# Graph attention on one core: where GpSimd issues late moves, adjacency loads and the accumulator base

## The reference

```python
h = relu(layernorm(x))
adj = maximum(adj, eye)
q, k, v = (einsum('nd,hdk->hnk', h, W) for W in (Wqs, Wks, Wvs))
scores = einsum('hqk,hmk->hqm', q, k) * 64 ** -0.5
scores = scores + 0.01 * eye - 1e16 * (1.0 - adj)
att = softmax(scores, axis=-1)
return x + einsum('hqm,hmk,hko->qo', att, v, Wo)
```

## Time and profile before

| | us |
|---|---|
| median of 3 runs | 2705.91 |
| lowest, highest | 2703.6, 2707.09 |
| the profiled execution's own time | 2709.6 |
| its span in the trace | 2708.1 |

### The profile page before, as it was taken

One profiled execution on the slowest core, in us unless ns is written; L12 is line 12 of the kernel. 1 busy time (PEld: TensorE's weight loads), 2 busy tenths in 40 slices (PEclk: granted clock), 3 DMA queues, 4 the chain that ended last, 5 costly groups with the idle time before them and its releaser, 6 DMA issues. The chain is left out here.

```text
span 2708.1 us, 58752 instructions
## 1 busy us (share of the span) xinstructions
PE 2630.7 (97%) x17344; PEld 1901.9 (70%) x17344; DVE 2253.6 (83%) x3833; ACT 1850.8 (68%) x3041; POOL 1280.6 (47%) x2418
## 2 busy tenths in 40 slices
PE   7899999999999999999998999999999999999997
PEld 5666777767777776766766777777777777777775
DVE  6788888888888888888847888888888888888885
ACT  3576777767767676776745777777777777777774
POOL 2356655566565556655512444444444444343433
PEclk9999999999999999999999999999999999999999
DMA  6367766677776677776652566656565656555654
GB/s 163 111 143 177 184 163 175 165 168 167 173 190 170 164 177 166 171 171 169 167 142 76 146 158 151 158 142 145 138 151 145 164 146 162 133 146 138 157 144 106
DMA packets 263358, 418.51 MB, mean 155 GB/s; under 512 B 98944, under 2 KB 119936, under 8 KB 259200
## 3 DMA queue, kind: packets, MB, share of 16 engines
q1 hardware_dynamic: 172032, 228.88, 33.0%
q0 software_dynamic: 89088, 184.69, 29.7%
q10 hardware_dynamic: 2176, 4.19, 0.4%
HBM read 136.31 MB, written 46.27 MB: 67 GB/s over the span
## 5 line engine op out<-in xcount | busy, mean ns | idle before, releaser
L307 POOL DMA_DIRECT2D S<-S x2048 | 1007.8, 500 | 1137.1 <-DVE S L723 1089.6
L702 DVE CUSTOM_DVE_ANT_0 S<-psS,B 128x1024 f32<-128x1024 f32 x1024 | 1228.4, 1218 | 268.3 <-PE psS L449 155.1
L589 ACT ACTIVATE S<-S,negm 128x1024 f32<-128x1024 f32 (+1 forms) x768 | 1095.8, 1428 | 88.8 <-DVE negm L709 88.3
L596 ACT ACTIVATE PT<-psT 128x512 f32<-128x512 f32 x1024 | 595.0, 596 | 267.5 <-PE psT L462 248.5
L449 PE MATMUL psS<-K,QH 128*128 128x512 f32 x2048 | 729.2, 437 | 35.7 <-DVE mx L702 31.5
L449 PE MATMUL psS<-K,QL 128*128 128x512 f32 x2048 | 642.5, 395 | 0.0
L462 PEld LDWEIGHTS psT<-ident,S 128*128 128x128 f32 x4096 | 481.2, 140 | 192.0 <-issue 73.5
L462 PE MATMUL psT<-ident,S 128*128 128x128 f32 x4096 | 608.0, 276 | 7.8 <-ACT S L589 4.9
L723 DVE STREAM_TRANSPOSE S<-S 128x2048 f32<-128x2048 f32 x256 | 590.2, 2306 | 27.6 <-PE psO L486 23.7
L472 PE MATMUL psO<-PT,V 128*64 128x256 f32 x4096 | 492.1, 382 | 0.0
L486 PE MATMUL psO<-S,V 128*64 128x256 f32 x4096 | 470.3, 382 | 2.0 <-DMA S<-S 2.0
(11 more groups left out here) (51 smaller groups left out, 967.9 us busy)
## 6 DMA issues: line engine op xcount, KB each, us to landing
S<-S SPq DMA_DIRECT2D x2048, 64.0 KB, 3.1
S<-S POOLq DMA_DIRECT2D x2048, 64.0 KB, 2.9
B<-in_adj POOLq DMA_DIRECT2D x128, 256.0 KB, 7.2
bias_scratch<-B SPq DMA_DIRECT2D x32, 1024.0 KB, 5.8
B<-bias_scratch SPq DMA_DIRECT2D x128, 256.0 KB, 5.1
hq<-hT_scratch SPq DMA_DIRECT2D x32, 256.0 KB, 3.5
RB<-rden_scratch SPq DMA_DIRECT2D x128, 64.0 KB, 3.2
S<-in_x SPq DMA_DIRECT2D x8, 512.0 KB, 3.6
```

Of the source, the lines that this page charges most:

```text
L307: pool.dma_start(dst, src).then_inc(late_sent[q][half], 16)
L589: nc.scalar.activation(part, part, ACT.Exp, bias=negm[:, h % 2, q:q + 1], accum_out=sums[:, h % 2, q, e:e + 1]).then_inc(probs_ready, 1)
L596: nc.scalar.activation(PT[:, s % RING, :], psT[s % 2][:, :], ACT.Copy).then_inc(pt_act, 1)
L702: nc.vector.tensor_tensor_reduce(out=part, in0=psS[j % 2][:, :], in1=B[:, q, k * SLOT:(k + 1) * SLOT], scale=SCALE, scalar=LOWEST, op0=ALU ...
```

## The change

In GpSimd's third step the moves of both query tiles now come first, then the wait for the store, then all four adjacency loads for tile 0, and the conversions and loads for tile 1 as they were. The two conversions of tile 1's first slots leave the end of the third step and stand in the fourth step between tile 0's and tile 1's moves. The base load moves from the third step to the second, behind the store. The old wait for the store protected `res`, among others; a new semaphore `res_free`, raised in the third step after that wait, is now waited for by VectorE's last add.

```diff
+    res_free = sem(f"res_free{g}")
...
+        pool.sem_inc(res_free, START)
...
             move_late(i, h, 0)
-            if adj_step:
+            if adj_rest:
                 for k in range(2):
-                    load_adj(i + 1, 0, k)
+                    convert(i + 1, 1, k, own_slot)
             move_late(i, h, 1)
-            if adj_step:
-                for k in range(2, SPT):
-                    load_adj(i + 1, 0, k)
             if prev and h == 1:
                 store(i - 1)
+                load_base(i)
             if prev and h == 2:
                 pool.wait_ge(stored, i * 16)
-                load_base(i)
+                pool.sem_inc(res_free, 1)
             if adj_step:
+                for k in range(SPT):
+                    load_adj(i + 1, 0, k)
                 for half_ in range(2):
...
-                for k in range(2):
-                    convert(i + 1, 1, k, own_slot)
...
+            if h == GROUP - 1:
+                dve.wait_ge(res_free, i + START)
```

## The result

| | before | changed |
|---|---|---|
| median of 15 runs, us | 2706.6 | 2713.0 |
| ratio, 95% interval | | 1.0033 (1.0024 to 1.0041) |
| span of the profiled execution | 2708.1 | 2711.5 |

The change makes the kernel slower by 0.33%, or 9 us by the ratio; the forecast was 2690 us, so the sign was wrong. One execution of before, at 7242 us, lies outside everything else, and the median is given for that reason. The two spans differ by 3.4 us only, since the profiled execution of before (2709.6 us) was 3 us longer than its median.

A forecast was written before the change was run, and what follows sets the result against it. TensorE (97% busy) and VectorE (83%) bound it; reordering GpSimd could only cut their waits. Gains of 13 us (group 0's order) and 3 us (base load) gave 2693.6 profiled, 2690 us as median; own range 2681 to 2700, widened to 2670 to 2714.

The forecast's parts named there:

- the ruler: The starts of the late transposes, two in every step: group 0 takes 0.57 us a step more than group 1.
- pair: Third and fourth steps of a four-step block, timed by late transposes; group 0 forecast to fall from 41.22 to 40.35 us.
- the floor of 38.54 us: Time of the two steps without loads in group 0's block 4, taken as the least the other two could take.
- Third step: Group 0: moves ahead of loads end slot 7's 1.92 us wait; the next step's transpose comes 1.8 us earlier.
- T2: Start of the first late transpose for head 2, where a block's third step begins; 459.36 us in block 4 before.
- L: Landing of the second adjacency load after the change, taken as 478.6 us in block 4; GpSimd's conversions follow.
- the chain: GpSimd's conversions, loads and moves from L on, 19.4 us in sum, ending at 498.0 against 498.09 before.
- Nothing else in it binds: Fourth step, group 0: only the last conversion limits it; tile 0's moves start at 484.9 (now 488.08) and land in time.
- The slower rival (c): Group 0: the loads' late start makes conversions the bound, pair 42.15 us, 2717 us in all; chance 0.15.
- The base load: Moved out of the crowded third step: at most 8 us to win in group 1, 3 us taken.
- The page's landing time: Estimate of 3.2 us for one adjacency load reading 512 KB, against 4.5 us at best in the trace.
- the rival that rested on early loads: Group 0: loads land early, TensorE becomes the limit, pair 39.15 us, 2672 us in all; chance 0.20.

The follow-up runs named there:

- e10: e5 with one of tile 0's adjacency loads put back ahead of tile 1's moves in the third step; 2670.5 us.
- e6: The changed kernel with each adjacency load after the first block bringing half the bytes; 2669.1 us.
- e8: The kernel before with each adjacency load after the first block bringing half the bytes; 2671.3 us.
- e7: The changed kernel with each conversion in the loop taking half a slot, all bytes still loaded; 2717.5 us.
- e5: The changed kernel with tile 1's first two loads right behind tile 0's four, the last two behind the first two conversions; 2678.8 us.
- e1: The kernel before with only the base load moved to the second step, and res_free; 2699.6 us.
- e2: The kernel before with only the new order of moves, loads and conversions, the base load staying in the third step; 2720.7 us.
- e4: The kernel before with only two conversions moved between the fourth step's moves, loads left as they were; 2712.5 us.
- e3: The kernel before with only both tiles' moves put ahead of all four loads, conversions left where they were; 2723.6 us.
- e11: e5 with the last two loads issued in the fourth step behind tile 0's moves; 2722.3 us.
- e12: e10 with two loads ahead of tile 1's moves in place of one; 2687.8 us.

## Why the prediction was wrong

**What bounds the kernel, the ruler, the places of the waits:** right. Group 0's pair has both the loss and, in e10, the gain; the floor of 38.54 us is the one near which group 1 (38.6), e6 (38.9) and e8 (38.6) stop.

**Third step:** right in kind and nearly in size. 1.8 us expected, 21.43 to 19.89 us measured, 1.5. In blocks 1 to 14 two masks still wait for moves there. In block 4 slot 7 still waits 2.1 us, as SyncE began its moves 1.1 us later there. One reading was off: the prediction put slot 7's wait down to GpSimd's moves of the earlier trace rows. In the kernel before these had landed by T2 + 17.7 in block 4, and SyncE's by + 19.5; the mask followed at + 19.8. The gain came because SyncE's moves, too, land earlier without loads ahead of them (the last at T2 + 17.3 and not + 19.6, means).

**L and the chain:** right. L was put at T2 + 19.2 and is 18.0 to 19.4 in the blocks; the chain was to end at T2 + 38.7 and ends at 37.3 in block 8. The prediction's care went into these numbers, and none of them decides. The way to L has a slip: 473.8 + 4.6 + 0.8 is 479.2 and not 478.6, which would have left 0.3 us of the pair's gain of 0.87. The measured L (T2 + 18.5 in the mean) is nearer the 478.6 (T2 + 19.2), and that is luck.

**"Nothing else in it binds: tile 0's moves start ... and land in time."** This is the step that failed. The start was right (T2 + 25.5 forecast, 24.7 measured). The landing was given no number at all. The earlier trace rows had shown that moves issued with loads ahead of them take 5.6 to 6.5 us to land and not 3.2 to 3.8; the same rule, used for the third step to claim the gain, was not used for the fourth, where four loads now stand right ahead of the moves. The prediction's own numbers would have shown it: slot 4 needs the first four of these moves; the fourth is issued at 486.4, and with 5.6 to 6.5 us it lands at 492.0 to 492.9, 1.3 to 2.2 us after the 490.7 at which slot 4 could be masked. Measured, they took 5.8 to 6.7 us in block 8, and slot 4 waits 1.7 us a block. Counted from the landings the masks of slots 4 to 7 wait 2.95 us a block for moves, where it was 1.36 (the profile's own attribution has 2.40 and 1.37 over blocks 1 to 14), and the fourth step gives back 2.03 us of which I had expected 0.9: the gain of 13 us in group 0 became a loss of 9.8.

**The slower rival (c)** had the sign and the place and the wrong mechanism: waits for a conversion are 0.10 us a block (blocks 1 to 14), and e7 shows that faster conversions don't help. Its "against" was also wrong in the same way, as it looked at the landing of loads and not at what the loads do to the moves.

**The late and torn stream of loads** was in no part of the sum. The change moves four loads 4.7 us later and leaves the other four behind conversions, so by T2 + 22 the DMA engines have passed 0.3 MB less than before, more than one load's 256 KB; the last load lands 1.1 us later, and so do tile 1's moves. The hole of 2 us is not new in itself, as the kernel before has one; but e5, which closes it, wins back 1.8 us a pair. A sum by engine, without the DMA engines as one of the engines, can't see it.

**The base load** was mis-sized: 3 us of a possible 8 in group 1; it is 7.2 us there by the transposes, and 0.6 us a pair in group 0 as well (e1, e2), which I had not counted at all. **res_free** costs nothing that shows: e1 has it and is not slower. The wait for the store, moved ahead of the loads, costs nothing either: the moves' issue ends at T2 + 11.4 and the first load is issued at + 11.6.

**The page's landing time.** No full load came near the 3.2 us that follows from the Trainium skill, "DMA: Bandwidth & Descriptors", section "Anatomy of one DMA — SWDGE (gpsimd) path"; the quickest of any run took 4.1 us, and the rival that rested on early loads did not come in.

## What to carry to other kernels

Where the DMA engines are near full over a stretch, put them into the sum as an engine of its own: list what each step has to pass, in order of issue over all queues, and price a moved transfer by what is queued behind it. An issue can be late in two ways, by delaying its own data and by leaving a hole that what stands behind it may pay for. Look for the hole in the kernel before as well, and for whether anything waits behind it. Where an instruction needs the transfers of two queues, read the landings of both; loads whose buffers are free should be issued ahead of the work that only their predecessors' data allows. And when a rule read from a row carries a gain in one step, apply it to the step that receives the displaced work.

## What the runs showed of the hardware

- Moves issued earlier into DMA engines at a share of 1.0 or more gain little, and the other queue's moves pay for it (means of 15 blocks, tile 0, fourth step): in e4 against before GpSimd's start 2.9 us earlier and land 1.2 us earlier, SyncE's land 1.5 us later; in e2 against e3 it is 4.0, 1.1 and 2.4 us.
- The moves of SyncE's queue wait for GpSimd's loads too: with the base load of 256 KB taken out of the third step of group 1, SyncE's last move of tile 1 landed at T2 + 17.3 us and not + 18.5 (medians of 14 blocks), GpSimd's own at + 16.3 both times, and the masks' waits for moves fell from 16.7 to 3.1 us in the whole group. In e11, with two loads issued between the two tiles' moves, SyncE's last move of tile 0 landed 5.2 us after GpSimd's (means).
- The second of two loads ahead of eight moves costs 1.5 us of the step (19.97 to 21.47 us, e12), the first one 0.26 us (19.71 to 19.97, e10).
- A mask that waited for moves starts 0.27 to 0.37 us after the landing of the last one (medians by slot, before and changed).
